# First-norm statistics ten tiles ahead, the scale chain in four pieces, three instructions for the routing places

## What is computed

```python
x = x + tanh(g_xattn[0]) * attention(ctx_1024, layernorm(x))   # 16 heads of 8; k, v from layer_norm(ctx), q from layer_norm(layernorm(x))
x = x + tanh(g_ffn[0]) * experts(layernorm(x))
# experts: gates = sigmoid(xf @ Wg); top 2 of 8, weights divided by their sum
#   shared = silu(xf @ Ws1) * (xf @ Ws3) @ Ws2, routed likewise per expert (128 -> 256 -> 128)
#   out = (shared + routed) / 3
```

## Time and profile before

| | |
|---|---|
| Median of 3 runs | 495.66 us (494.84 to 497.26) |
| The profiled execution's own time | 495.87 us |
| Its span in the profile | 494.1 us |
| PE busy | 371.6 us (75%), 3462 instructions |
| DVE busy | 348.9 us (71%), 886 instructions |
| ACT busy | 265.6 us (54%), 601 instructions |
| POOL busy | 304.3 us (62%), 367 instructions |
| Mean granted TensorE clock | 0.862 of full |

### The profile page before, as it was taken

One profiled execution on the slowest core, in us unless ns is written; L12 is line 12 of the kernel. 1 busy time (PEld: TensorE's weight loads), 2 busy tenths in 40 slices (PEclk: granted clock), 3 DMA queues, 4 the chain that ended last, 5 costly groups with the idle time before them and its releaser, 6 DMA issues.

```text
span 494.1 us, 10185 instructions
## 1 busy us (share of the span) xinstructions
PE 371.6 (75%) x3462; PEld 274.1 (55%) x3462; DVE 348.9 (71%) x886; ACT 265.6 (54%) x601; POOL 304.3 (62%) x367
## 2 busy tenths in 40 slices
PE   0669797988779775879876984089999999999600
PEld 0347465755456543656564863067777777777400
DVE  2449787887979869669977586047776677776537
ACT  1438577584467643638636561045665655666334
POOL 4364658575478795779945677401777777777710
PEclk9989889797798977859959895579999999999955
DMA  4900589791000111000000112621333666751169
GB/s 118 289 20 3 211 341 366 299 391 71 12 23 25 34 37 41 17 19 23 23 23 24 33 50 100 237 77 53 92 108 130 238 222 219 253 197 53 48 223 303
DMA packets 39330, 62.33 MB, mean 126 GB/s; under 512 B 5936, under 2 KB 23344, under 8 KB 39280
## 3 DMA queue, kind: packets, MB, share of 16 engines
q1 hardware_dynamic: 32704, 51.12, 30.0%
q0 software_dynamic: 4992, 10.30, 6.2%
...
## 4 chain that ended last, share of the span: by engine, by line
PE 42%; POOL 23%; DVE 13%; issue 13%; ACT 4%; DMA 3%; SPq 0%; POOLq 0%; DVEq 0%; ACTq 0%
POOL expert_rows L543 8%; PE ps L1199 6%; PE ps L1201 5%; PE ps L1200 5%; POOL k_mask L577 5%; PE ps L1110 4%; PE ps L1142 4%; PE ps L1236 3%; POOL token_sums L610 3%; POOL scale_in L554 2%; PE ps L1131 2%; PE ps L1224 2%; PE ps L1222 2%; PE ps L1223 2%; DVE inv_sum L967 2%
## 5 line engine op out<-in xcount | busy, mean ns | idle before, releaser
L610 POOL DMA_INDIRECT token_sums<-prob,y_at x92 | 94.6, 1028 | 60.4 <-DVE prob L1026 38.5
L577 POOL TENSOR_TENSOR k_mask<-k_st,head_mask 128x1024 f32<-128x1024 f32 x32 | 61.0, 1907 | 52.5 <-ACT k_st L682 52.3
L543 POOL DMA_INDIRECT expert_rows<-c_sb,pos x64 | 64.2, 1002 | 17.0 <-issue 16.7
L726 ACT ACTIVATE h_hi<-prob 128x512 fp32r<-128x512 f32 x62 | 38.2, 632 | 37.3 <-DVE prob L989 37.3
L719 ACT ACTIVATE probT<-ps 128x512 f32<-128x512 f32 x62 | 36.9, 599 | 30.0 <-PE ps L1201 27.0
L926 DVE TENSOR_REDUCE row_max<-ps 128x16 f32<-128x1024 f32 x32 | 39.0, 1218 | 16.8 <-PE ps L1110 16.6
L989 DVE TENSOR_TENSOR prob<-ps,probT 128x512 f32<-128x512 f32 x62 | 40.2, 684 | 13.1 <-ACT probT L719 10.2
L1103 PE MATMUL ps<-ident,norm 128*128 128x128 f32 x32 | 11.4, 356 | 50.0 <-DVE norm L891 25.7
L690 ACT ACTIVATE probT<-ps 128x512 f32<-128x512 f32 x64 | 35.5, 595 | 16.4 <-PE ps L1142 16.4
L1110 PE MATMUL ps<-k_mask,qT 64*64 64x512 f32 x256 | 43.8, 761 | 0.0
L994 DVE TENSOR_TENSOR h_lo<-prob,h_hi 128x512 fp32r<-128x512 f32 x62 | 40.5, 689 | 3.4 <-ACT h_hi L726 0.4
...
## 6 DMA issues: line engine op xcount, KB each, us to landing
...
```

The lines of the kernel that those rows point to most:

```text
L543: pool.indirect_dma_start(out=xs, out_offset=bass.IndirectOffsetOnAxis(pos[:, k, i:i + 1], 0), in_=c_sb[:, i, :], in_offset=None).then_inc ...
L577: pool.tensor_tensor(k_mask[:, m, :, :, :], k_st[:, m, :, :].unsqueeze(2).broadcast_to(shape), head_mask[:, :].unsqueeze(1).unsqueeze(3).b ...
L610: pool.indirect_dma_start(out=ys, out_offset=bass.IndirectOffsetOnAxis(y_at[:, s, k:k + 1], 0), in_=yrows[:, s % 2, k * D:(k + 1) * D], in ...
L726: act.activation(h_hi[:, n % 2, f, :], h[:, f, :], ACT.Copy).then_inc(h_hi_done, 1)
```

## The change

- The statistics run further ahead: tiles 4 to 11 are done in steps -2 to 1, two per step, and then tile t + 10 in step t. The number of instructions is the same.
- `scale_first(k)` gets a second argument, the part. The chains of groups 0 and 1 run all four parts in a row (ahead of the loop, and in step 0). Those of groups 2 to 7 run one part in each of four successive steps, from step 2 on, after the step's `w_lo` and ahead of its scatter. The power over 8 columns (both inputs of four tiles) is split into one of 4 columns for x, in part 0, and one of 4 for the context, in part 3.
- `places` has three instructions where seven were: one product of the counts with both picks, one reduction, one conversion to integers. The experts' first rows (`region`) are no longer added: `carry` begins with e x T/128 for expert e instead of 0, and the matmul with ones in `count_before` makes e x T of it.
- `slot_table` compares the totals with a table that holds each expert's base too (`steps512`, 8 x 7 numbers instead of 7).

```diff
--- before.py
+++ after.py
@@ -143,15 +143,14 @@
         gate_tmp = sb("gate_tmp", [P, 5, GT * E])
         chosen = sb("chosen", [P, E * GT])
         so_far = sb("so_far", [P, E * GT])
-        place = sb("place", [P, E * GT])
+        place_of = sb("place_of", [P, 2, GT])
         carry = sb("carry", [P, NG + 1, E])
         pos = sb("pos", [P, 2, NT], I32)
         ones = sb("ones", [P, P])
         not_before = sb("not_before", [P, P])
         zeros = sb("zeros", [P, ZROWS * XW])
         begins = {n: sb(f"begins{n}", [P, E * n]) for n in (4, 8)}
-        region = sb("region", [P, E])
-        steps512 = sb("steps512", [P, JMAX - 1])
+        steps512 = sb("steps512", [P, E, JMAX - 1])
         earlier = sb("earlier", [P, E, E])
         slot_id = sb("slot_id", [P, DYN])
         slot_less = sb("slot_less", [P, DYN])
@@ -398,9 +397,9 @@
 
         def stats_tiles(t):
 
-            if t < 1:
-                return {-2: [4, 5], -1: [6], 0: [7]}.get(t, [])
-            return [t + 7] if t + 7 < NT else []
+            if t < 2:
+                return {-2: [4, 5], -1: [6, 7], 0: [8, 9], 1: [10, 11]}.get(t, [])
+            return [t + 10] if t + 10 < NT else []
 
         @block.sync
         def _(sp):
@@ -520,7 +519,8 @@
                 pool.memset(earlier[:, :, :], 1.0)
                 for b in begins.values():
                     pool.memset(b[:, :], 1.0)
-                pool.memset(carry[:, 0, :], 0.0).then_inc(table_step, 1)
+                pool.iota(carry[:, 0, :], [[T // P, E]], base=0, channel_multiplier=0,
+                          allow_small_or_imprecise_dtypes=True).then_inc(table_step, 1)
                 pool.wait_ge(table_step, 2)
                 pool.affine_select(out=not_before[:, :], in_=not_before[:, :], compare_op=ALU.is_ge, fill=0.0, base=0,
                                    pattern=[[-1, P]], channel_multiplier=1)
@@ -529,8 +529,7 @@
                 for n, t in begins.items():
                     pool.memset(t[:, :].rearrange("p (e t) -> p e t", e=E)[:, :, 0:1], 0.0)
                 exact = dict(channel_multiplier=0, allow_small_or_imprecise_dtypes=True)
-                pool.iota(region[:, :], [[T, E]], base=0, **exact)
-                pool.iota(steps512[:, :], [[ROWS, JMAX - 1]], base=ROWS, **exact)
+                pool.iota(steps512[:, :, :], [[T, E], [ROWS, JMAX - 1]], base=ROWS, **exact)
                 pool.iota(slot_id[:, :], [[1, DYN]], base=0, **exact)
                 pool.iota(slot_less[:, :], [[1, DYN]], base=1 - JMAX, **exact).then_inc(tables_ready, 1)
 
@@ -543,28 +542,36 @@
                     pool.indirect_dma_start(out=xs, out_offset=bass.IndirectOffsetOnAxis(pos[:, k, i:i + 1], 0),
                                             in_=c_sb[:, i, :], in_offset=None).then_inc(scattered, 16)
 
-            def scale_first(k):
-
-                pool.wait_ge(aggr_done, (k + 1) * LB)
+            def scale_first(k, part):
+
                 o = slice(k * LB % MVS, k * LB % MVS + LB)
-                var_c_x, one = mv[:, o, :, 1], scale_in[:, o, 1]
-                pool.tensor_tensor(var_eps[:, :, :], var_c_x, eps[:, :, :], ALU.add).then_inc(scale_step, 1)
+                one = scale_in[:, o, 1]
                 at = k * SC + 1
-                pool.wait_ge(scale_step, at + 1)
-                pool.tensor_tensor(scale_in[:, o, :], var_eps[:, :, :], minus_half[:, :, :],
-                                   ALU.pow).then_inc(scale_step, 1)
-                pool.wait_ge(scale_step, at + 2)
-                pool.tensor_tensor(var_x[:, :], mv[:, o, 1, 1], one, ALU.mult).then_inc(scale_step, 1)
-                pool.wait_ge(scale_step, at + 3)
-                pool.tensor_tensor(var_x[:, :], var_x[:, :], one, ALU.mult).then_inc(scale_step, 1)
-                pool.wait_ge(scale_step, at + 4)
-                pool.tensor_tensor(var_x[:, :], var_x[:, :], eps[:, :, 0], ALU.add).then_inc(scale_step, 1)
-                pool.wait_ge(scale_step, at + 5)
-                pool.tensor_tensor(rstd_b[:, :], var_x[:, :], minus_half[:, :, 0], ALU.pow).then_inc(scale_step, 1)
-                pool.wait_ge(scale_step, at + 6)
-                pool.tensor_tensor(one, rstd_b[:, :], one, ALU.mult).then_inc(scale_ready, 1)
-
-            SC = 6
+                if part == 0:
+                    pool.wait_ge(aggr_done, (k + 1) * LB)
+                    if k > 0:
+                        pool.wait_ge(scale_ready, k)
+                    pool.tensor_tensor(var_eps[:, :, :], mv[:, o, :, 1], eps[:, :, :], ALU.add).then_inc(scale_step, 1)
+                    pool.wait_ge(scale_step, at + 1)
+                    pool.tensor_tensor(one, var_eps[:, :, 1], minus_half[:, :, 1], ALU.pow).then_inc(scale_step, 1)
+                if part == 1:
+                    pool.wait_ge(scale_step, at + 2)
+                    pool.tensor_tensor(var_x[:, :], mv[:, o, 1, 1], one, ALU.mult).then_inc(scale_step, 1)
+                    pool.wait_ge(scale_step, at + 3)
+                    pool.tensor_tensor(var_x[:, :], var_x[:, :], one, ALU.mult).then_inc(scale_step, 1)
+                    pool.wait_ge(scale_step, at + 4)
+                    pool.tensor_tensor(var_x[:, :], var_x[:, :], eps[:, :, 0], ALU.add).then_inc(scale_step, 1)
+                if part == 2:
+                    pool.wait_ge(scale_step, at + 5)
+                    pool.tensor_tensor(rstd_b[:, :], var_x[:, :], minus_half[:, :, 0], ALU.pow).then_inc(scale_step, 1)
+                    pool.wait_ge(scale_step, at + 6)
+                    pool.tensor_tensor(one, rstd_b[:, :], one, ALU.mult).then_inc(scale_step, 1)
+                if part == 3:
+                    pool.wait_ge(scale_step, at + 7)
+                    pool.tensor_tensor(scale_in[:, o, 0], var_eps[:, :, 0], minus_half[:, :, 0],
+                                       ALU.pow).then_inc(scale_ready, 1)
+
+            SC = 7
 
             def step(t, b):
                 m = 1 - b
@@ -593,9 +600,11 @@
                     s = w_slice(t)
                     pool.tensor_tensor(w_lo[:, s], w_raw[:, (t - WS_FROM) % RING, :], w_hi[:, s].bitcast(F32),
                                        ALU.subtract).then_inc(w_split, 1)
-                for i in stats_tiles(t):
-                    if i % LB == LB - 1:
-                        scale_first(i // LB)
+                if t == 0:
+                    for part in range(4):
+                        scale_first(1, part)
+                if t >= 2 and (t + 6) // LB < NT // LB:
+                    scale_first((t + 6) // LB, (t + 6) % LB)
 
                 if t == 0:
                     tables()
@@ -621,7 +630,8 @@
                 if n >= TURN_FROM and slot_of(n - 1) is not None:
                     scatter_sums(n - 1)
 
-            scale_first(0)
+            for part in range(4):
+                scale_first(0, part)
             attention_steps(step, lambda: None, unit)
             expert_units(unit)
 
@@ -837,18 +847,14 @@
 
                 t0, t1 = GROUPS[g]
                 tiles, m = slice(t0, t1), t1 - t0
-                pick1, pick2, key = (by_tile(gate_tmp[:, k, 0:m * E]) for k in (2, 3, 4))
-                at = place[:, 0:E * m].rearrange("p (e t) -> p e t", e=E)
+                both = [P, 2, m, E]
+                picks = gate_tmp[:, 2:4, 0:m * E].rearrange("p k (t e) -> p k t e", e=E)
+                at = gate_tmp[:, 0:2, 0:m * E].rearrange("p k (t e) -> p k t e", e=E)
                 dve.wait_ge(ranked, g + 1)
-                then(dve.tensor_tensor(at, p_rank[:, 0:E * m].rearrange("p (e t) -> p e t", e=E),
-                                       region[:, :].unsqueeze(2).broadcast_to([P, E, m]), ALU.add))
-                at = place[:, 0:E * m].rearrange("p (e t) -> p t e", e=E)
-                then(dve.tensor_tensor(key, at, pick1, ALU.mult))
-                then(dve.tensor_reduce(rank[:, tiles], key, AX_X, ALU.add))
-                dve.tensor_copy(pos[:, 0, tiles], rank[:, tiles])
-                then(dve.tensor_tensor(key, at, pick2, ALU.mult))
-                then(dve.tensor_reduce(share[:, tiles], key, AX_X, ALU.add))
-                dve.tensor_copy(pos[:, 1, tiles], share[:, tiles]).then_inc(pos_ready, 1)
+                then(dve.tensor_tensor(at, p_rank[:, 0:E * m].rearrange("p (e t) -> p t e", e=E).unsqueeze(1)
+                                       .broadcast_to(both), picks, ALU.mult))
+                then(dve.tensor_reduce(place_of[:, :, 0:m], at, AX_X, ALU.add))
+                dve.tensor_copy(pos[:, :, tiles], place_of[:, :, 0:m]).then_inc(pos_ready, 1)
 
             def shares():
 
@@ -864,7 +870,7 @@
                     return v.unsqueeze(axis).broadcast_to(shape)
                 dve.wait_ge(totals_ready, 1)
                 then(dve.tensor_tensor(cmp_j[:, :, :], over(p_totals, [P, E, JMAX - 1], 2),
-                                       over(steps512[:, :], [P, E, JMAX - 1], 1), ALU.is_gt))
+                                       steps512[:, :, :], ALU.is_gt))
```

## The result

The changed kernel takes 473.95 us (median of 4 runs, 473.15 to 474.72) beside 496.34 us for the kernel before on the same chip: ratio 0.955, 95% interval 0.952 to 0.958, 22.4 us less. The profiled execution took 473.69 us with a span of 471.8 us, so its own difference of span is 22.3 us.

What follows compares the result with a forecast made beforehand. Ordinary attention steps were taken as bound by VectorE (5.54 us), with GpSimd's scale chains adding waits and clock falls, and scatter steps by GpSimd. Gains less costs sum to 23.1 us: 495.7 - 23.1 = 472.6, range 469 to 481 (0.81).

Steps and rivals of the forecast that it cites:

- steps 4 to 13: Attention steps before the scatters: pieces fit GpSimd's idle time, VectorE bounds each step at 5.54 us; gain 13.9 us.
- 14 and 15: VectorE's first routing batch, 17.4 us: only some waits for a slow TensorE go; gain 0.7 us.
- 16 and 17: Attention steps of 15.1 us together that lose a chain and a part of places; gain 2.5 us.
- 18 to 21: First scatter steps, bound by GpSimd, where a piece hides behind nothing: 29.1 us instead of 31.3; gain 2.2 us.
- 24 to 26: Scatter steps after VectorE's second routing batch: 22.1 us instead of 25.8; gain 3.7 us.
- start, to step 4: First chain 0.46 us dearer on the path, and step 0 with the larger table 0.2 us dearer.
- behind the last key mask: Later routing: the shorter places of step 33 lies on the chain of waits; gain 0.8 us.
- Rivals 3: Steps 4 to 13 stay at 6.93 us because the clock keeps falling for another reason: 486.5 us; chance 0.06.
- Rival 4: Steps 4 to 13: clock low for long makes TensorE the bound, slower, 523 us if always low; chance 0.03.
- Rival 1: Scatter stage: TensorE idles, its clock falls, GpSimd waits for the transposed tile; 6.5 us lost, 479 us; chance 0.13.
- my middle value for step 26: Third step of steps 24 to 26, 7.5 us before: taken as 6.5 us, between 6.09 and 7.5.
- Rival 2: A power on GpSimd holds VectorE in steps 4 to 13: up to 8.2 us, 480.8 us; chance 0.10.

Runs made afterwards that it cites:

- e3: The changed kernel with all four parts of a chain run in one step again, statistics still ten tiles ahead: 485.62 us, ratio 0.985.
- e1: The kernel before with only the three-instruction places, carry and larger slot table; chains and statistics as before: 489.07 us, ratio 0.991.
- e5: The changed kernel without the chains of groups 2 to 5 (steps 2 to 17): 475.53 us, ratio 0.961.
- e6: The changed kernel with an idle power of 4 columns added on GpSimd in each of steps 4 to 13: 478.95 us, ratio 0.966.
- e7: The changed kernel with two idle bn_stats added on VectorE in each of steps 4 to 13: 480.16 us, ratio 0.969.
- e2: The changed kernel with the old seven-instruction places: 475.26 us, ratio 0.962.

## Why the prediction was right, and where it was not

The predicted 472.6 us stand beside 473.95. The terms are off by up to 1.3 us, some one way and some the other, and it is in part luck that the gain came out within 0.7 us of the 23.1. The terms of the sum came out so (gain in us, predicted and measured in the profiled execution):

| term | predicted | measured |
|---|---|---|
| steps 4 to 13 | 13.9 | 12.7 |
| 14 and 15 | 0.7 | 0.1 |
| 16 and 17 | 2.5 | 2.7 |
| 18 to 21 | 2.2 | 2.75 |
| 22 and 23 | 0 | 0 |
| 24 to 26 | 3.7 | 5.0 |
| start, to step 4 | -0.7 | -1.1 |
| behind the last key mask | 0.8 | 0.1 |
| sum | 23.1 | 22.3 |

- **Steps 4 to 13.** The mechanism held: no drop of the clock, hardly a wait before `c_sb`, and key masks about 5.6 us apart. The size was 1.2 us off: the step of 5.54 us from 73.59 was taken as VectorE's own work, the same in every step. It was one in which no norm was held. In the changed kernel such steps take 5.41 (from 64.94 and 70.35) to 5.66 us, and those of steps 4 to 6, where `w_lo` holds an instruction each time, 5.69 to 5.83. That the pieces cost nothing there came out. What the sum didn't have is a second, slower rhythm of these steps, 2.0 us longer, into which one kernel with fewer pieces and one with an added power fell. Rivals 3 and 4 fell with the full clock from 48 to 105 us. Rival 4's argument, that falls of the clock follow stops of 2 us or more, isn't what the traces show: the kernel before fell (from 150 on) after a stop of 1.6 us at 146.4, and the changed kernel stopped for 2.2 us at 157.0 and kept its clock.
- **Where the 12.7 us came from.** The prediction put the whole on the chain as one thing. The runs divide it: 6.5 us by the pieces (e3 against the changed kernel), 3.3 by the earlier statistics (e3 against e1), and 2.9 that e1 has as well, with one fall of the clock less. What the clock's falls cost in the other two parts no run separates.
- **Steps 18 to 21.** 28.6 us beside 29.1 predicted, GpSimd never waiting for the key. The run without late chains gives 24.6 (from the steps of 6.09 it would be 24.4), so "behind nothing" was nearly right: 3.9 us of 4.45.
- **Steps 24 to 26.** Rival 1's fear and my middle value for step 26 were both too high: step 26 took 6.06 us, and GpSimd didn't wait for the transposed tile in it. The gain was 5.0. But the same stretch is 1.5 us longer in e5, e6 and e7 and 2.5 in e2, where step 26 takes 7.5, so this term is good to 2 us or so.
- **Steps 14 and 15.** The batch still stops TensorE and halves its clock (117 to 124). I had counted 0.7 us of a slow TensorE as gone, and that was wrong.
- **The places.** 0.79 us instead of the 0.75 assumed, and 0.73 in step 33 (243.11 to 243.84). That they gave some 0.9 us ahead of the tail shows there, but not in the total: from the last key mask to the last scatter the kernels need 69.8 to 73.2 us with the same work, by where the clock falls in it. Taken alone they gave 4.4 us (3.0 to 6.2), more than the 1.8 that the instructions account for; the rest is of the size of the 2.9 us in steps 4 to 13, which go with the clock.
- **Rival 1 (TensorE starves in the scatter stage)** fell: full clock from 124 to 175 us, and then a fall only behind the second routing batch, where TensorE had stopped for 5.7 us. A stretch of that stage, in which TensorE worked 21.3 of 28 us and kept the clock:

```profile
135.00:163.00 28.00, 21.29 (x345) 15.24 (x344) 27.83 (x62) 19.15 (x52) 25.71 (x32) 1.00 0.12 37
```

- **Rival 2 (a power holds VectorE)** fell. Line 986, the former 980 of the earlier trace rows, has the same durations:

```profile
L986 DVE TENSOR_SCALAR var_eps<-mv x32: 132/141/154, 47.4 to 247.7; 128x1 f32<-128x1 f32 x32
```

Nor is a norm held: in the 14 kernels 78 instructions of VectorE on 128x128 elements (line 946 and the norms) begin beside a power of 4 columns (1.02 us), and they take 0.33 to 0.38 us. Twelve of them are in the kernel before, at 55.23 and 55.47 for instance, where this rival could have been decided. Yet VectorE is held: not by the powers, but by `w_lo`, which was there before the change.
- **The start.** 1.07 us instead of 0.7. The first chain cost 0.35, step 0 0.12 and steps 1 and 2 the rest, in a stretch where the clock was low (31.8 to 38.7).
